# First MLP layers as seven block products instead of eight, in an fp32-by-parts attention, MLP and adapter kernel on one Trainium2 core

## The reference

```python
q, k, v = x @ Wq, x @ Wk, x @ Wv
attn_out = softmax(q @ k.T * 512 ** -0.5) @ v @ Wp + bp
cms      = gelu(attn_out @ cW1 + cb1) @ cW2 + cb2 + one_hot(code)      # 512 -> 2048 -> 512
modifier = gelu(concat(attn_out, cms) @ mW1 + mb1) @ mW2 + mb2         # 1024 -> 2048 -> 512
y   = clip(x + cms + modifier, 0, 1)
out = layer_norm(y + gelu(y @ W_down[s] + b_down[s]) @ W_up[s] + b_up[s]) * ln_w[s] + ln_b[s]
```

## Time and profile before

| | before |
| --- | --- |
| device time, median of 3 runs | 1147.96 us (1147.32 to 1148.12) |
| device time of the profiled execution | 1147.69 us |
| its span, first to last instruction | 1145.9 us |
| PE busy | 1128.0 us (98%), 5024 matmuls |
| DVE, ACT, POOL busy | 603.5, 351.0, 168.3 us |
| mean granted PE clock | 0.998 |
| first MLP unit starts / first adapter matmul starts | 213.6 us / 1082.6 us |

### The profile page before, as it was taken

How to read it: one execution, slowest core, us unless ns; L and a number is a source line. 1 busy time by engine, 2 the same in 40 slices (tenths; PEclk the granted TensorE clock), 3 DMA queues, 4 the chain that set the end, 5 groups by cost and what they waited for, 6 DMA issues and landing times.

```text
span 1145.9 us, 13657 instructions
## 1 busy us (share of the span) xinstructions
PE 1128.0 (98%) x5024; PEld 933.1 (81%) x5024; DVE 603.5 (53%) x931; ACT 351.0 (31%) x616; POOL 168.3 (15%) x123
## 2 busy tenths in 40 slices
PE   7999999999999999999999999999999999999996
PEld 6888888788888888888888888888888888888885
DVE  3734334365665566566874444444445453435667
ACT  3624323323322332232521212121212121212575
POOL 0501101101111111110111111000111110101014
PEclk9999999999999999999999999999999999999999
DMA  7301100012121111210000000000000000000723
GB/s 258 111 1 37 37 1 19 19 47 71 49 64 60 59 64 46 73 55 29 28 29 28 28 27 1 27 27 27 27 27 27 27 0 27 27 27 38 274 83 120
DMA packets 47536, 58.16 MB, mean 51 GB/s; under 512 B 3984, under 2 KB 28560, under 8 KB 46480
## 3 DMA queue, kind: packets, MB, share of 16 engines
q1 hardware_dynamic: 46928, 56.67, 14.7%
q10 hardware_dynamic: 576, 1.05, 0.3%
HBM read 47.22 MB, written 10.49 MB: 50 GB/s over the span
## 4 chain that ended last, share of the span: by engine, by line
PE 95%; DVE 3%; ACT 1%; DMA 0%; issue 0%; DVEq 0%; ACTq 0%
PE bank L429 32%; PE bank L430 31%; PE bank L431 31%; DVE z L942 1%; DVE stats L936 1%; PE bank L473 1%; ACT res L709 0%; DMA WqT_raw<-WqT_dram 0%; DVE mean_var L938 0%; DVE attn_lo L929 0%; ACT L748 0%; DVE rstd L945 0%; ACT gelu_f L742 0%; ACT L742 0%; ACT L680 0%
## 5 line engine op out<-in xcount | busy, mean ns | idle before, releaser
L866 DVE TENSOR_TENSOR res<-bank,res 128x512 f32<-128x512 f32 x240 | 163.9, 692 | 262.7 <-PE bank L431 262.7
L680 ACT ACTIVATE gelu_f<-bank,hidden_bias 128x512 f32<-128x512 f32 x128 | 88.3, 690 | 627.0 <-PE bank L431 626.9
L866 DVE TENSOR_TENSOR cms_acc<-bank,cms_acc 128x512 f32<-128x512 f32 x240 | 163.4, 692 | 121.2 <-PE bank L431 121.2
L383 POOL TENSOR_TENSOR wsplit<-raw,wsplit 128x512 fp32r<-128x512 f32 (+1 forms) x76 | 117.1, 1541 | 741.6 <-ACT wsplit L614 626.1
L429 PE MATMUL bank<-gelu_hi,wsplit 128*128 128x512 f32 x512 | 199.4, 389 | 0.8 <-DVE gelu_lo L852 0.8
L430 PE MATMUL bank<-gelu_lo,wsplit 128*128 128x512 f32 x512 | 199.2, 389 | 0.0
L431 PE MATMUL bank<-gelu_hi,wsplit 128*128 128x512 f32 x512 | 199.2, 389 | 0.0
L429 PE MATMUL bank<-attn_hi,wsplit 128*128 128x512 f32 x512 | 199.2, 389 | 0.0
L430 PE MATMUL bank<-attn_lo,wsplit 128*128 128x512 f32 x512 | 199.2, 389 | 0.0
L431 PE MATMUL bank<-attn_hi,wsplit 128*128 128x512 f32 x512 | 199.2, 389 | 0.0
L429 PEld LDWEIGHTS bank<-gelu_hi,wsplit 128*128 128x128 f32 x512 | 96.1, 188 | 21.4 <-DVE gelu_lo L852 1.5
(11 more groups left out here) (119 smaller groups left out, 1160.6 us busy)
## 6 DMA issues: line engine op xcount, KB each, us to landing
raw<-cW_dram SPq DMA_DIRECT2D x32, 256.0 KB, 2.9
raw<-mW_dram SPq DMA_DIRECT2D x16, 512.0 KB, 4.2
experts_split<-wsplit SPq DMA_DIRECT2D x24, 256.0 KB, 2.8
res<-xT_dram SPq DMA_DIRECT2D x4, 1024.0 KB, 8.4
x_raw<-x_dram SPq DMA_DIRECT2D x4, 1024.0 KB, 5.6
raw<-mW_dram SPq DMA_DIRECT2D x16, 256.0 KB, 4.4
cms_hi<-experts_split SPq DMA_DIRECT2D x4, 1024.0 KB, 4.9
cms_lo<-experts_split SPq DMA_DIRECT2D x4, 1024.0 KB, 7.0
```

The lines of the kernel that those rows point to most:

```text
L383: pool.tensor_tensor(dst, src, f32(hi), ALU.subtract).then_inc(done, 1)
L680: act.activation(dst[:, g, :], bank[r][:, :], ACT.Gelu, bias=hidden_bias[:, s:s + 1]).then_inc(gelu_made, 1)
L866: op = dve.tensor_tensor(dst, src, dst, ALU.add)
```

## The change

The hidden layer is now done in *groups* instead of units. A group g is two 128-wide hidden blocks by two batches: 16 groups of cms (pairs of batches in turn, g even is batches 0 and 1, g odd is 2 and 3), then 16 of the modifier (g 16 to 23 for batches 0 and 1, g 24 to 31 for batches 2 and 3). Within a group the first layer is a 2 x 2 by 2 x 2 block product over (hidden blocks) x (halves of the contraction) x (batches), in the Strassen-Winograd form: seven block products `product_part(g, 0..6)`, whose operands are the blocks or their sums and differences T1 to T4 (right side, `xo` for attn_out and `co` for cms) and S1 to S4 (left side, POOL's `sums_13`, `sum_2`, `sum_4`). One block product has half the contraction: 6 matmuls in cms, 12 in the modifier (`sources` [0] or [0, 1]). The seven are gathered in banks 0 to 2 and in SBUF tiles by one ACT copy (`keep_first`) and five DVE additions (`join`).

The second layer (`out_tiles(g, h)`, h the batch of the pair) sums both hidden blocks of the group in PSUM before DVE adds it (`add_outputs`): two contraction steps per tile, 24 matmuls for four tiles.

SBUF no longer holds all at once: the operands of batches 2 and 3 (`x1_kept`, 14 tiles of 512 KB), cms of batches 2 and 3 (`cms_kept`) and y of batches 0 and 1 (`y_kept`) go to DRAM and come back. cms and x of batches 0 and 1 are added to the modifier's sum from `staged` tiles. The adapter pieces are 24 of 128 KB, in groups 2 to 13, two in each. The second weights of the modifier have one buffer (`second(w)`, `k = 1` for w >= 8).

The order on PE (P0 to P6 the block products, O0 and O1 the `out_tiles` of the group before):

```diff
+            for g in range(GROUPS):
+                if g == MOD0:
+                    for i in range(3):
+                        product_part(g, i, [0], last=False)
+                    out_tiles(g - 1, 0)
+                    out_tiles(g - 1, 1)
+                    for i in range(3):
+                        product_part(g, i, [1], first=False)
+                    for i in range(3, 7):
+                        product_part(g, i, [0, 1])
+                    continue
+                sources = [0, 1] if is_mod(g) else [0]
+                for i in (0, 1):
+                    product_part(g, i, sources)
+                if g > 0:
+                    out_tiles(g - 1, 0)
+                for i in (2, 3, 4):
+                    product_part(g, i, sources)
+                if g > 0:
+                    out_tiles(g - 1, 1)
+                for i in (5, 6):
+                    product_part(g, i, sources)
```

and what they wait for:

```diff
+            def product_part(g, i, sources, first=True, last=True):
+                bank_i = bank[(0, 1, 2, 0, 1, 1, 2)[i]]
...
+                    if i < 3 and g > 0:
+                        if i == 0:
+                            pe.wait_ge(gelu_made, 2 * gelus(g - 1, C11))
+                        else:
+                            pe.wait_ge(joined, joins(g - 1, JC21 if i == 1 else JC12))
+                    elif i == 3:
+                        pe.wait_ge(s1_made, g + 1)
+                    elif i > 3:
+                        pe.wait_ge(joined, joins(g, (U2, U3, JC22)[i - 4]))
...
+            def out_tiles(g, h):
+                w = second_set(g)
+                hi, lo, _ = second(w)
+                pe.wait_ge(W2_made, w + 1)
+                pe.wait_ge(gelu_lo_made, gelus(g, C12 if h else C21))
...
+                for m in range(KT):
+                    if outputs(g, h, m) > KT:
+                        pe.wait_ge(summed, outputs(g, h, m) - KT)
+                    product(bank[4 + m][:, :], [((hi[:, n, cols(m)], lo[:, n, cols(m)]), (H_hi[:, c, :], H_lo[:, c, :]))
+                                                for n, c in enumerate((C12, C22) if h else (C11, C21))]).then_inc(out_filled, 1)
```

DVE's order in a group (the special groups 0, 16, 23 and 24 put sums and `lo` parts of whole operands, 1024 elements a partition, between these; C11, C21, C22, C12 are the four gelu tiles of a group):

```diff
+                    gelu_low(g - 1, C21)
+                    gelu_low(g - 1, C12)
...
+                    if g == 24:
+                        for op in (T2, T1, T3):
+                            co_lo(1, op)
+                    join(g, U2)
+                    if g == 0:
+                        for op in (T2, T1, T3):
+                            xo_lo(op)
+                    else:
+                        add_outputs(g - 1, 0)
...
+                    if g > MOD0:
+                        add_staged(g, outputs(g - 1, 0, KT - 1))
+                if g == 23:
+                    co_sum(1, T1)
+                    co_sum(1, T2)
+                join(g, U3)
+                join(g, JC22)
+                gelu_low(g, C11)
...
+                if g > 0 and g != MOD0:
+                    add_outputs(g - 1, 1)
...
+                join(g, JC21)
+                gelu_low(g, C22)
+                join(g, JC12)
```

ACT's order (`gelu` is two activations, hi first; `gelu(g, C22)` and `gelu(g, C12)` also wait for O1, `left_hi(.., i)` for product i of the set that it overwrites):

```diff
+                if g > 0:
+                    gelu(g - 1, C12)
+                for s, t in splits_in(g - 1) if g > 0 else []:
+                    left_hi(s, t, 6, g - 1)
...
+                keep_first(g)
...
+                for i in (0, 1):
+                    for s, t in sets:
+                        left_hi(s, t, i, g)
+                if not is_mod(g) and sets and sets[0][1] < 8:
+                    second_hi(sets[0][1])
+                if g in PIECE_GROUPS:
+                    piece_to_hi(2 * (g - 2))
...
+                gelu(g, C11)
...
+                gelu(g, C22)
+                if g in PIECE_GROUPS:
+                    piece_to_hi(2 * (g - 2) + 1)
...
+                gelu(g, C21)
...
+                for s, t in sets:
+                    left_hi(s, t, 5, g)
...
+                if is_mod(g):
+                    second_hi(second_set(g))
```

SP's order in the cms groups, and the condition of the second weights:

```diff
+            for g in range(MOD0):
+                if g % 2 == 0:
+                    load_left(0, g // 2 + 1)
+                if g == MOD0 - 2:
+                    load_left(1, 0)
+                if g == 2:
+                    for i in range(7):
+                        sp.wait_ge(xo_made[1][i], 1)
+                        for half in range(2):
+                            sp.dma_start(x1_kept[i, half], f32(flat(xo[1][i][half][:, :, :]))).then_inc(x1_saved, 16)
+                if g in PIECE_GROUPS:
+                    split_piece(2 * (g - 2))
+                if g % 2 == 0 and g // 2 + 1 < 8:
+                    load_second(g // 2 + 1)
+                if g in PIECE_GROUPS:
+                    split_piece(2 * (g - 2) + 1)
...
+            def load_second(w):
...
+                    sp.wait_ge(out_filled, outputs(2 * w - 3 if w < 8 else MOD0 + w - 9, 1, 3))
...
+            def split_piece(u):
+                e, part = u // PARTS, u % PARTS
+                if u > 0:
+                    sp.wait_ge(piece_saved, 32 * u)
+                sp.dma_start(piece_raw[:, :], adapter[e, part]).then_inc(piece_loaded, 16)
+                sp.wait_ge(piece_lo_made, u + 1)
+                for half, tile in enumerate((piece_hi, piece_lo)):
+                    sp.dma_start(experts[e, half, :, 256 * part:256 * (part + 1)], f32(tile[:, :])).then_inc(piece_saved, 16)
```

More of the change, by code:

```diff
@@ L260, in layers_kernel @@
[L260 to L267, removed]
+        PIECE_GROUPS = range(2, 2 + PIECES // 2)
+        X_CHECK = GROUPS - 9
+        CO_HI_ORDER = [(B11, B21, T1, T2, T4, T3, B22), (B11, T2, T3, T4, T1, B21, B22)]
+        XO_HI_ORDER = (T1, T2, T3, T4)
         block = ctx.enter_context(nc.Block())
@@ new lines, in _ @@
+            for b in range(B - 1):
+                split_xn(b)
+            pool.wait_ge(xT_lo_made, KT * B)
+            pool.wait_ge(lo_made, pos[2, "F", 3] + 1)
+            xo_sum(0, T2, B22, T1)
+            xo_sum(0, T3, B22, T3)
+            pool.wait_ge(xo_step[0], 1)
+            xo_sum(0, T4, B21, T2)
+            pool.wait_ge(xo_step[0], 3)
+            for op in (B11, B21, B22):
+                xo_lo(0, op)
+            split_xn(B - 1)
+            for op in (T2, T1):
+                xo_lo(0, op)
@@ new lines, in _ @@
+            sums_13(0, 0)
+            left_lo(0, 0, 0)
+            sum_2(0, 0)
+            for i in (1, 2, 3):
+                left_lo(0, 0, i)
+            sum_4(0, 0)
+            for i in (4, 5, 6):
+                left_lo(0, 0, i)
+            second_lo(0)
+            for op in (T3, T4):
+                xo_lo(0, op)
+            pool.wait_ge(lo_made, LAST + KT)
+            xo_lo(1, B11)
+            pool.wait_ge(xo_step[1], 3)
+            for op in (B21, T4, B22):
+                xo_lo(1, op)
@@ new lines, in gelu @@
+            def gelu(g, c):
+                n = 2 * n_pair(g) + (c in (C22, C21))
+                column = (MB1 if is_mod(g) else CB1) + n
+                src = {C11: bank[0], C22: u3_t, C21: s1_t, C12: u2_t}[c][:, :]
+                f = gelu_f[:, :] if c == C11 else src
+                if c == C11:
+                    act.wait_ge(made, products(g, 3))
+                    if g > 0:
+                        act.wait_ge(gelu_lo_made, gelus(g - 1, C11))
+                else:
+                    act.wait_ge(joined, joins(g, {C22: JC22, C21: JC21, C12: JC12}[c]))
+                if g > 0:
+                    act.wait_ge(out_filled, outputs(g - 1, c in (C22, C12), KT - 1))
+                for dst in (H_hi[:, c, :], f):
+                    act.activation(dst, src, ACT.Gelu, bias=bias[:, column:column + 1]).then_inc(gelu_made, 1)
@@ L723, in _ @@
[L723 to L730 removed]
+                    if b < 2:
+                        act.wait_ge(y01_lo_made, 2 * b + m // HALF + 1)
+                    else:
+                        act.wait_ge(y_lo_made, KT * (b - 2) + m + 1)
```

996 lines of the change are left out of this document (659 added, 337 removed).

## The result

The changed kernel takes **1139.99 us** (median of 5 runs, 1136.54 to 1140.76) against 1147.96 us (1147.32 to 1148.21) for the kernel before: a ratio of 0.9923, 95% interval 0.9903 to 0.9943. So it is faster by 8 us, not by the 20 forecast. The profiled execution took 1140.68 us, its span 1138.4.

A forecast was written before the change was run, and what follows sets the result against it. PE, busy 98% of the span, was taken as the bound: -65.3 + 9 + 13 + 6 + 8 + 8 + 1 = -20.3 us from 1147.69 gives 1127.4, predicted as 1128 us, whole range 1105 to 1148.

The forecast's parts named there:

- Bound, count and pitch: Whole kernel: PE bounds it; 288 fewer matmuls at 0.2266 us each save 65.3 us.
- Plain groups cost nothing: Plain cms and modifier groups: PE waits 0, with slack of 1.1 us in cms and 1.5 in the modifier.
- Rivals 3 (second-weight chain): Modifier groups: the single second-weight buffer's chain misses O0, 3.3 us late in 15 groups costing 27, 1155 us; chance 0.12.
- 4 (POOL starves DVE): Modifier groups: POOL's unbroken rows delay U3, 1 us in 15 groups and twice that at transitions, 1146 us; chance 0.08.
- Start +9: Group 0 of the MLPs: P4 waits 3 us and P5 6 on DVE's sums and lo parts; bounds 5 and 13.
- Saves +13: The first piece waits behind group 2's 14 saves, so O0 of group 3 starts at 36, not 23: 13 us.
- Rival 1: Saves and small loads share the engines, so pieces are not held; the 13 and 6 go, 1109 us; chance 0.21.
- Second pieces +6: Even cms groups 4 to 12: the second piece, issued after the second weights, delays O0 by 1.2 us each, five times.
- Cms to modifier +8: Groups 15 and 16: DVE sums and lo parts, output additions and late second weights cost 8 us; bounds 3 and 15.
- group 24 +8: Change of the batch pair: T2's lo part comes late for P1, 7.5 us, taken as 8; bounds 4 and 13.
- Tail +1: From the first adapter matmul on: 1 us for second weights behind 2 MB of adapter weights; bounds -1 and 4.
- Rival 2: Joins and transitions hide too: starts at their low bounds and no piece waits, 1094 us; chance 0.08.

The follow-up runs named there:

- e2: The changed kernel with 138 spare matmuls, their results unread, ahead of PE's eight longest waits: 1133.76 us, ratio 0.9874 against the kernel before.
- e1: The kernel before with 60 chained small DVE copies ahead of one gelu lo in the modifier, so that PE waits once: 1161.96 us, ratio 1.0120.
- e9: The kernel of e1 with 50 spare matmuls ahead of PE's wait: 1159.66 us, ratio 1.0101 against the kernel before.
- e7: The changed kernel with POOL's four long lo parts for batches 2 and 3 replaced by fills with zero: 1129.86 us, ratio 0.9840 against the kernel before.
- e4: The changed kernel with the 14 saves moved from group 2 to groups 5 to 11, two in each: 1128.15 us, ratio 0.9825 against the kernel before.
- e5: The changed kernel with the second piece's load issued ahead of the second weights' load in even cms groups: 1130.88 us, ratio 0.9852 against the kernel before.
- e6: The changed kernel with T2's lo part made ahead of gelu C12's lo on DVE in group 24: 1136.81 us, ratio 0.9893 against the kernel before.
- e11: The changed kernel with saves, piece loads, and DVE work in groups 0, 1, 16, 24 reordered, second weights split earlier in groups 16 and 23: 1099.41 us, ratio 0.9576.

## Why the prediction was wrong

The failed step is the sum: it has no term for TensorE's granted clock. The text named a clock under 1.00 behind the long wait as what would make it wrong, and gave it no price, on the ground that the only lower row was 0.90 in the idle tail. The profiled execution missed by 13.3 us (1140.68 against 1127.4). Of these, 10.5 are distances between 0.3 and 0.72 us, where the text had nothing, and e2 takes 9.3 of them away as half rate. That it is the clock and that idle PE brings it is shown by e1 and e9; what it is worth here, 6 us net, by e2. So even at full clock the change would have given 14 and not 20: the rest of the 13.3 is 1.4 us more wait than the 44 summed (46.3 less 0.9 of before), 0.8 each in the attention and in other distances and 0.5 around the span, less 0.7 in the tail; and of the 10.5, 1.2 stay at full clock as the first distance behind each wait (e2), and of the 9.3 that go, 3.1 come back as waits.

Point by point:
- **Bound, count and pitch**: right. 288 fewer matmuls at 0.2266.
- **Plain groups cost nothing**: right (the chain that the text adds to 22.0 is 21.9, slack 1.2); 160.00 us of PE busy in 160.00. Rivals 3 (second-weight chain) and 4 (POOL starves DVE) did not come, although `gelu_low` did grow from a mean of 0.835 us to 1.106 in the largest of its groups by shape:

```profile
L1325 DVE TENSOR_TENSOR H_lo<-u_t,H_hi 128x512 fp32r<-128x512 f32 x64 | 70.8, 1106 | 24.6 <-ACT u_t L1046 24.6
```

- **Start +9**: right in sum (9.9), the long wait under-priced by the port (8.2 against 6): POOL's `lo` parts do not keep their 2.4 us and DVE's take 3.2 (e7).
- **Saves +13**: 11.1, in the right place and with ACT standing on the piece (e4). Rival 1, that the pieces are not held up, is refuted; whether the transfers ahead or SP's own issuing hold them is open.
- **Second pieces +6**: 7.6, removed whole by e5.
- **Cms to modifier +8** and **group 24 +8**: 8.0 and 8.8, each on the instruction named (P1 of group 24 was due at 32.6 by the text's own clock, 29.9 + 2.7, and not at 33.1). What the steps left out is that the one of group 24 stood in front of another: the wait on W_lo that e6 uncovered.
- **Tail +1**: 0.3.
- **Rival 2** (starts and transitions hide) is refuted by the wait list.

The sum of the waits was foretold within 1.4 us, in part by luck: the single steps are off by up to 1.9 us and partly cancel (the saves 1.9 too dear, the second pieces 1.6 too cheap). The price of having waited was left out.

## What to carry to other kernels

When an edit puts waits on an engine that was always busy, price each long one twice: its length, and the work behind it at the lower clock. Here one 11.5 us wait cost 2.3 more, and 46 us of waits at fifteen places some 9, of which about 6 could be had back by keeping PE busy. And before judging a reduction of work by its time, put the in-order queues right: which load stands behind which saves, and which short `lo` behind which long one. The arithmetic here saved 65 us; the order that it came with let 8 of them show, and that of e11 let 49.

## What the runs showed of the hardware

- Behind the waits of 6.99, 8.19 and 8.80 us the granted clock was 0.50 to 0.51 and some 5, 10 and 13 matmuls started 0.43 us apart; behind 3.28 and 3.18, 9 and 6; behind the five waits of 1.2 to 1.7 us none. The Trainium skill, TensorE: Matmul & The Clock Gate, "Wait — 56ns, not 53.3ns?", gives 426.7 ns between two matmuls of 512 columns at the lower clock; the trace agrees (0.43).
- The number differs between executions with the same instructions: group 3 had 5 half-rate matmuls in the changed kernel and 22 in e6, twelve of these behind a wait of 1.3 us. So the length of the wait just before them does not say how many follow. The runs of the changed kernel spread over 4.2 us, those of e1, with one long wait, over 1.1, and those of e9, where it is filled, over 0.6. That the first causes the second was not tested.
- A POOL subtraction of 1024 elements does not keep its 2.40 us when DVE runs several with two SBUF inputs in a row: the two take turns, and both are lengthened (DVE's to 3.19). POOL's timeline at the start of the changed kernel:

```profile
216.22 3.45 POOL L552 TENSOR_TENSOR x_B_lo<-x_B_f,x_B_hi 128x1024 fp32r<-128x1024 f32 x1 [6.72 <-DVE x_B_f L1203]
221.97 2.38 POOL L552 TENSOR_TENSOR x_B_lo<-x_B_f,x_B_hi 128x1024 fp32r<-128x1024 f32 x1 [2.30 <-DVE x_T_f L1279]
224.31 3.32 POOL L552 TENSOR_TENSOR x_T_lo<-x_T_f,x_T_hi 128x1024 fp32r<-128x1024 f32 x1
```
